# Performer attention: squared norms by full eight-column products, and the queries' norm subtracted together with their maximum

## What is computed

```python
def softmax_kernel(data, proj, is_query, eps=0.0001):
    dn = data.shape[-1] ** (-0.25)
    ratio = proj.shape[0] ** (-0.5)
    dd = jnp.einsum('bhnd,md->bhnm', data * dn, proj)
    diag = jnp.sum(data * data, axis=-1, keepdims=True) * 0.5 * (dn * dn)
    if is_query:
        mx = jnp.max(dd, axis=-1, keepdims=True)
    else:
        mx = jnp.max(dd, axis=(-1, -2), keepdims=True)
    return ratio * (jnp.exp(dd - diag - mx) + eps)
```

## Time and profile before

| | |
|---|---|
| median of three runs | 10747.63 us |
| lowest and highest | 10739.18, 10761.16 us |
| the profiled execution | 10741.04 us |
| its span, first to last instruction | 10739.2 us |
| granted TensorE clock over the span | 0.946 |
| first key feature products (`c_P<-c_W,c_t`) start | 5385.7 us |
| last query norm products (`c_P<-c_qsq,c_kon`) start | 9130.3 us |

### The profile page before, as it was taken

One profiled execution on the slowest core, in us unless ns is written; L12 is line 12 of the kernel. 1 busy time (PEld: TensorE's weight loads), 2 busy tenths in 40 slices (PEclk: granted clock), 3 DMA queues, 4 the chain that ended last, 5 costly groups with the idle time before them and its releaser, 6 DMA issues. The chain is left out here.

```text
span 10739.2 us, 163898 instructions
## 1 busy us (share of the span) xinstructions
PE 9045.1 (84%) x58878; PEld 4711.9 (44%) x58878; DVE 7542.2 (70%) x8522; ACT 6059.0 (56%) x12480; POOL 5837.1 (54%) x3881
## 2 busy tenths in 40 slices
PE   7888888988888777577688889989898998799987
PEld 3333333333333333466655555555555554433334
DVE  5999999999999998566566665555666564344442
ACT  4666667666676665111166666666666666333333
POOL 5888889888988887566433333322332331024441
PEclk8999999999999999788798999999999999899998
DMA  2222222222222222666500000000000000300004
GB/s 71 77 78 74 80 80 79 77 80 79 80 77 79 77 78 75 187 197 199 162 1 1 5 2 5 5 1 5 1 5 1 5 2 10 138 1 1 1 1 145
DMA packets 259098, 623.58 MB, mean 58 GB/s; under 512 B 26279, under 2 KB 114447, under 8 KB 255992
## 3 DMA queue, kind: packets, MB, share of 16 engines
q1 hardware_dynamic: 203672, 438.27, 12.5%
q0 software_dynamic: 51840, 169.91, 5.4%
q10 hardware_dynamic: 2784, 4.92, 0.1%
HBM read 572.09 MB, written 40.90 MB: 57 GB/s over the span
## 5 line engine op out<-in xcount | busy, mean ns | idle before, releaser
L978 POOL TENSOR_TENSOR a_dBu<-a_du,a_Bs 128x960 f32<-128x960 f32 (+1 forms) x1280 | 2714.6, 2144 | 222.0 <-DVE a_H L750 202.0
L750 DVE TENSOR_TENSOR_SCAN a_H<-a_pA,a_dBu 128x962 f32<-128x962 f32 (+1 forms) x1280 | 2654.7, 2074 | 107.6 <-ACT a_pA L919 56.4
L919 ACT ACTIVATE a_pA<-a_delta,a_al 128x480 f32<-128x480 f32 (+1 forms) x2560 | 1624.8, 639 | 1148.0 <-DVE a_H L750 1143.1
L541 PE MATMUL a_pY<-a_H,cst 128*128 128x480 f32 (+1 forms) x5120 | 2211.7, 553 | 34.4 <-ACT a_Y L936 34.1
L758 DVE TENSOR_TENSOR a_H<-a_H,a_pC 128x960 f32<-128x960 f32 (+1 forms) x1280 | 1396.1, 1091 | 81.4 <-PE a_pC L541 80.2
L541 PEld LDWEIGHTS a_pY<-a_H,cst 128*128 128x128 f32 x5120 | 975.1, 193 | 704.5 <-issue 538.5
L3433 POOL TENSOR_TENSOR e_P<-e_P 128x1024 f32<-128x1024 f32 (+1 forms) x240 | 454.5, 1918 | 958.3 <-ACT e_P L3404 953.8
L541 PE MATMUL a_pC<-a_stk,a_sel 96*128 96x480 bf16 (+1 forms) x1280 | 471.0, 368 | 514.6 <-DVE a_H L758 505.9
L1089 POOL DMA_INDIRECT b_gath<-b_tab,b_idx x648 | 613.2, 946 | 382.5 <-issue 175.8
L2459 POOL TENSOR_TENSOR c_KF<-c_KF,c_dg 128x1056 f32<-128x1056 f32 x192 | 386.0, 2011 | 673.5 <-DVE c_MX L2219 673.0
L3305 DVE TENSOR_REDUCE e_part<-e_slot 128x2 f32<-128x1024 f32 (+3 forms) x400 | 418.6, 1069 | 428.4 <-PE e_slot L3154 426.6
(11 more groups left out here) (481 smaller groups left out, 17678.6 us busy)
## 6 DMA issues: line engine op xcount, KB each, us to landing
a_Bs<-a_brows SPq DMA_DIRECT2D x512, 480.0 KB
a_Bs<-a_brows SPq DMA_DIRECT2D x128, 384.0 KB
d_W<-in_d_w SPq DMA_DIRECT2D x32, 1024.0 KB, 8.0
f_W<-in_f_w SPq DMA_DIRECT2D x32, 1024.0 KB, 7.7
b_tab<-b_TT SPq DMA_DIRECT2D x32, 576.0 KB
b_gath<-b_tab,b_idx POOLq DMA_INDIRECT x648
a_zt<-a_sz SPq DMA_DIRECT2D x36, 256.0 KB
a_sz<-a_zt SPq DMA_DIRECT2D x16, 480.0 KB
```

The source lines that it names most:

```text
L541: return pe.matmul(out, lhsT, rhs, start=start, stop=stop, skip_group_check=True)
L750: v.tensor_tensor_scan(span(H[:, g % NH, :], g), factors(g), span(dBu[:, g % ND, :], g), 0.0, ALU.mult, ALU.add).then_inc(S(kind), 1)
L919: s.activation(pA[:, k, at:at + z], delta[:, u % 2, h, 0:z], ACT.Exp, scale=al[:, o + 2 * d, h, n:n + 1]).then_inc(S(kind), 1)
L978: g.tensor_tensor(inner(dBu[:, i % ND, :], i), du[:, u % 2, :, 0:z], Bs[:, p % NB, i % 2, 0:z].unsqueeze(1).broadcast_to([128, 2, z]), ALU ...
```

## The change

Keys: the 12 products of 32 rows and two columns become three products of 128 rows and eight columns, one for each block of 128 positions, into columns 264 to 287 of the first bank. Queries: three such products of `qsq` are put at the end of `qd`, behind a wait for `q2`; VectorE adds the 24 norms to the 24 maxima before the split, so that the bf16 parts subtract both; the four products of 384 columns with `less` leave `qft`, and with them the wait for `q2` there. `q2` waits for the `qd` two chunks earlier in place of the `qft`. The half of PSUM that `qd` holds is given back after the addition. Four costs of the plan's table change: `kf` 1.5 to 1.05, `qd` .85 to .95, `qft` 1.5 to 1.1, and `q_max` 1.3 to 1.5. The constant `less` leaves its tile.

```diff
-            "kf": ("PE", 1.5), "kf_out": ("ACT", 1.3), ...
+            "kf": ("PE", 1.05), "kf_out": ("ACT", 1.3), ...
-            "qd": ("PE", .85), "q_max": ("DVE", 1.3), ... "qft": ("PE", 1.5),
+            "qd": ("PE", .95), "q_max": ("DVE", 1.5), ... "qft": ("PE", 1.1),
...
     def diag(kind, *key):
-        return half(kind, *key)[:, :, 264:270]
+        return half(kind, *key)[:, 0, 264:288]
+
+    def by_heads(t24):
+        return t24.rearrange("p (t i h) -> p i t h", t=3, i=4)
...
                     pe.wait_ge(S("k2"), upto("k2", n, c))
                     for t in range(3):
-                        for i in range(4):
-                            r = slice(32 * i, 32 * i + 32)
-                            m = mm(diag(kind, n, c)[:, i, 2 * t:2 * t + 2], t2[r, c % 2, t * 128:(t + 1) * 128],
-                                   d2[r, 2 * i:2 * i + 2])
+                        m = mm(diag(kind, n, c)[:, 8 * t:8 * t + 8], t2[:, c % 2, t * 128:(t + 1) * 128], d2[:, :])
...
                     for t in range(3):
                         for i in range(4):
                             r = slice(32 * i, 32 * i + 32)
-                            m = mm(p[:, i, t * 88:(t + 1) * 88], Q[r, n % 2, ts(c, t)], wsl(n, 1536, 88)[r, :])
+                            mm(p[:, i, t * 88:(t + 1) * 88], Q[r, n % 2, ts(c, t)], wsl(n, 1536, 88)[r, :])
+                    pe.wait_ge(S("q2"), upto("q2", n, c))
+                    for t in range(3):
+                        m = mm(diag(kind, n, c)[:, 8 * t:8 * t + 8], qsq[:, c % 2, t * 128:(t + 1) * 128], d2[:, :])
...
-                    pe.wait_ge(S("q2"), upto("q2", n, c))
-                    for i, r in enumerate(rows):
-                        mm(p[0:88, i, 0:CH], less[r, :], qsq[r, c % 2, :], False, False)
...
-                    v.tensor_reduce(mr[:, c % 2, :, :], heads("qd", n, c), AX.X, ALU.max).then_inc(S(kind), 1)
+                    v.tensor_reduce(mr[:, c % 2, :, :], heads("qd", n, c), AX.X, ALU.max).then_inc(S("q_most"), 1)
+                    v.wait_ge(S("q_most"), upto(kind, n, c))
+                    m24 = mr[:, c % 2, :, :].rearrange("p i (t h) -> p i t h", t=3)
+                    v.tensor_tensor(m24, m24, by_heads(diag("qd", n, c)), ALU.add).then_inc(S(kind), 1)
...
-                    s.activation(d24, diag("kf", n, c), ACT.Copy).then_inc(S("kf_diag"), 1)
+                    s.activation(d24, by_heads(diag("kf", n, c)), ACT.Copy).then_inc(S("kf_diag"), 1)
...
                     if prev:
-                        g.wait_ge(S("qft"), upto("qft", *prev))
+                        g.wait_ge(S("qd"), upto("qd", *prev))
```

More of the change, by code:

```diff
@@ L1314, in layer2a @@
     sincos = ph.sb("sincos", [128, 2, L])
-    kon = ph.sb("kon", [128, 3, 88])
+    kon = ph.sb("kon", [128, 2, 88])
     identh = ph.sb("identh", [128, 128], BF16)
@@ L1355, in layer2a @@
     MATES = [row ^ 1 for row in range(32)]
-    mask, sel, less = (kon[:, k, :] for k in range(3))
+    mask, sel = (kon[:, k, :] for k in range(2))
     turn, turn0, mean0 = hm[:, 0, :], hm[:, 1, :], hm[:, 2, :]
@@ L1390, in layer2a @@
             "k_sum": ("POOL", 1.03), "q_sum": ("POOL", 1.0), "k2": ("ACT", .52), "q2": ("POOL", .87),
-            "kf": ("PE", 1.5), "kf_out": ("ACT", 1.3), "kf_max": ("DVE", 1.2), "kf_less": ("POOL", 2.4), "pk_part": ("DVE", .46),
+            "kf": ("PE", 1.05), "kf_out": ("ACT", 1.3), "kf_max": ("DVE", 1.2), "kf_less": ("POOL", 2.4), "pk_part": ("DVE", .46),
             "pk_turn": ("PE", .15), "pk_most": ("DVE", .5), "pk_row": ("PE", .1), "pk_all": ("DVE", .18),
@@ L1394, in layer2a @@
             "ctx_mask": ("DVE", .9), "ctx_turn": ("PE", .25), "ctx_out": ("ACT", .38),
-            "qd": ("PE", .85), "q_max": ("DVE", 1.3), "q_split": ("DVE", .8), "mt": ("PE", .3), "mt_out": ("ACT", .49), "qft": ("PE", 1.5),
+            "qd": ("PE", .95), "q_max": ("DVE", 1.5), "q_split": ("DVE", .8), "mt": ("PE", .3), "mt_out": ("ACT", .49), "qft": ("PE", 1.1),
             "q_exp": ("ACT", 1.45), "den": ("PE", .7), "num": ("PE", .7), "inv": ("ACT", 1.15), "o": ("DVE", .61),
@@ L2353, in _ @@
                     n, c = key
-                    d24 = dg[:, c % 2, :].rearrange("p (i g) -> p i g", i=4)
+                    d24 = dg[:, c % 2, :].rearrange("p (i t h) -> p i t h", i=4, t=3)
                     s.wait_ge(S("kf"), upto("kf", n, c))
@@ L3534, in layout @@
     pick = (row % 2 == np.arange(88)[None] // 44).astype(f) * (row < 6)
-    a["c_kon"] = asc(np.stack([pair, -pick, f(-0.125) * pair], axis=1))
+    a["c_kon"] = asc(np.stack([pair, -pick], axis=1))
     a["c_d2"] = asc((np.arange(128)[:, None] // 16 == np.arange(8)[None]) * f(0.125))
```

## The result

The changed kernel takes 10827.58 us (median of four runs, 10825.25 to 10844.26) against 10743.4 us for the kernel before (four runs): 1.0076 times as long, 95% interval 1.0063 to 1.0089. That is 84 us more. The prediction was 10,820 us, 72 us more than the 10747.63 us known then, with a range from 10,680 to 10,890 us.

The account below looks back on a forecast made before the run. The prediction took TensorE to bound the Performer's loop, busy 90% of it. Records +22, addition +17, moved wait +8 and clock +25 summed to +72 us, giving 10,820 us against the median, range 10,680 to 10,890 us.

Parts of the forecast that it names:

- What bounds the kernel: Performer's loop: it goes at TensorE's pace, busy 90% of 3600 us, with 358 us standing still.
- Prices of records: TensorE's groups in `kf`, `qd` and `qft`: +0.13 us a chunk over 192 chunks, +22 us at the end.
- Three products for twelve save almost nothing: Keys' norms in `kf`: weight loads are what is paid for; group 0.67 us against 0.71, `kf` +0.07 us a chunk.
- The rule weighed there: Norm groups: about 60 cycles per matmul, estimated 0.15 us for six, forecast near 10,615 us; weighed and not adopted.
- The clock: Performer's loop: more thin TensorE time lengthens half-speed stretches; +25 us, between nothing and 58 us.
- The addition: VectorE after the maximum in `qd`: PSUM half freed 0.21 us later, for 83 waits; +17 us, bounds 0 and 40.
- The moved wait: TensorE waits for `q2` inside `qd`, holding up everything behind; five late squares, +8 us, bounds 0 and 16.
- rival 2: Planner's new order gives back a third of TensorE's 358 us idle, 120 us; 10,700 us, faster; chance 0.16.
- Cheap products: Six fp32 norm records in `kf` and `qd` take 0.34 us a group; 10,681 us, faster; chance 0.12.
- Covered: TensorE's additions fall into its waits, releases move along, clock holds; +10 us or so, 10,755 us; chance 0.15.
- waits for `c_qsq` under 16 us: Sign in the later timeline: TensorE's waits for GpSimd's square of the queries at or under 16 us.
- `c_mr` waits above 108 us: Sign in the later timeline: waits on the queries' maximum longer than 108 us in all.

Follow-up runs that it names:

- code_only: The change without its four new planned costs, so the work order stays that of before; 1.0105 times the kernel before.
- keys_only: The kernel before with only the keys' three full norm products put into `kf`, queries and plan untouched; 0.9999 times the kernel before.
- norm_out: Order of before and the change's `kf`, but no queries' norm computed: `less` products removed, nothing put in, no addition; 0.9944 times the kernel before.
- no_add: The changed instructions in the order of before, without VectorE's addition of norms to maxima; 1.0089 times the kernel before.
- old_wait: The changed instructions in the order of before, with `qd`'s norm products reading Q and `q2` waited for in `qft`; 1.0102 times the kernel before.
- norm_both: The kernel before with three unused full products of eight columns added at the end of `qd`, nothing taken out; 1.0135 times the kernel before.
- costs_only: The kernel before with only the four new planned costs, so old instructions in the changed kernel's order; 1.0006 times the kernel before.

## Why the prediction was right, and where it was not

**What bounds the kernel** held. In code_only the stage grew by 118 us, TensorE's busy time by 119, idle time by nothing.

**Prices of records** held. Norm group 0.69 us in `kf` and `qd`, 0.67 predicted; features with a change of form 0.85, predicted 0.84; a new exposed load behind them: the pair takes 0.73 us, and 0.65 undisturbed, 0.08 for 0.10. In `kf` that is 0.85 + 0.69 + 0.08 = 1.62 us, predicted 1.61. "Three products for twelve save almost nothing" is keys_only's 0.9999. The records' +22 us answer to 25 or 26 in code_only.

**The rule weighed there**, that of the Trainium skill, "TensorEngine Tiling (Array Packing)", section Instruction Overhead, does not describe the fp32 group: it takes 0.115 us a record. For bf16 records the trace comes near it: 0.09 us for three and 0.17 for six, 0.03 each, against the 0.025 us that the prediction estimated from the page's 60 cycles. Both forms have a load of their own for each product; its median is 192 ns in fp32 and 96 ns in bf16. The prediction put the price down to the load. That fits, but no run tells the load from another fixed cost of an fp32 record.

**The clock** was the step that failed, by its size: "I take +25 us, a little under the middle". code_only shows 188 us more at the lower level, 94 us, above even the upper bound of 58 us that the prediction set by scaling low stretches with thin time. In the change's own order the stage has 596 us of low-clock time for 423, a cost of 83 us. The scaling itself was the fault, for low stretches do not grow in proportion to thin time. norm_out has hardly more thin time than before (only that of `kf`), and has 46 us more at the lower level; code_only has 188 us more, where thin time up by 30% gave 129 at most. The stretch at 6549.70 is one place where the clock falls, `qd` behind a wait of 0.87 us with `down` to follow. How far each of wait, loads and missing columns counts, there and elsewhere, stays open.

**The addition**, +17 us: no_add gives 17 us with intervals that overlap, and 18 us of waits on the maximum, so right in size as far as it can be told. **The moved wait**, +8 us: 14 us of waits in code_only, no difference in time in old_wait; in the change's own order 1.5 us. Neither is seen in the sum, since the idle time of code_only is that of before. norm_both, where work alone was added, lost 43 us of idle time, so part of such waits is covered by the added work.

**The order** had no term in the forecast. It was rival 2, priced at -120 us for an order that gives back a third of the idle time. It gave back about 31 us, through 32 us less idle time; its 10 us less of clock and 12 us more of work are within what single executions scatter. So the nearness of 10,828 to 10,820 is partly luck. In the changed kernel's stage the forecast's +25 us for the clock came out as +83, its +25 us for the two waits as 33 us less idle time, and its +22 us of records as +38: two misses of 58 us each that cancel.

**The rivals.** Cheap products: against it, 0.69 us a group. Covered: against it as a whole, the idle time of code_only did not shrink and the clock fell, though norm_both shows that some covering takes place. Of the signs named beforehand, the group near 0.67 us, waits for `c_qsq` under 16 us and a clock of 0.93 or less (0.92 over the stage) were seen. `c_mr` waits above 108 us were seen too, with 124, but for another reason than the one meant: costs_only, without the addition, has them as well, and code_only, with it, has not.

## What to carry to other kernels

Count groups by their time from start to start, not by products: 24 records of 32 rows in four row groups side by side took 0.71 us and the six full fp32 records that replace them 0.69. So joining them saves nothing, while moving such a group into a place that had none costs its full 0.69 us. In fp32 a product of few columns cost as much as one of 128 (0.11 us a record), and bf16 parts are the cheap way: six records in 0.17 us for 0.71. Before moving work from a long streaming product to short ones, look at what follows them: the clock can fall there, and in the stretch shown the densely streamed work behind paid for it.

## What the runs showed that was not expected

Three bf16 records of 128 rows and eight columns take 0.09 us start to start, 0.03 each, against 0.057 for bf16 records of 128 columns and 0.115 in fp32. Taking 0.64 us a chunk of streamed columns out of `qft`, with nothing put in, raised low-clock time by 46 us, so less work for TensorE gave 23 us back to the clock and 25 to idle time. The sign chosen beforehand for the addition, the waits on the maximum, answered to the order and not to the addition.
